# Last mixer of a graph network: row statistics in two parts, and its first work moved into the attention slots

## The chip, the cores and the metric

The kernel runs on one core of a Trainium2 chip. The time is the device time of one execution in microseconds (us), as a median of several runs. The engines are TensorE (PE in the profile, its weight loads PEld), VectorE (DVE), ScalarE (ACT), GpSimd (POOL) and SyncE (SP); each runs its own instruction stream in order, and they meet through semaphores.

## What is computed

x is (64, 128, 128) in float32: 64 batches, 128 nodes, 128 features. Four mixers follow each other, each as x = x + mixer(relu(layernorm(x))). The first is two graph convolutions and four LSTMs over windows, the second graph attention, the third masked self attention, the fourth a spectral graph network:

```python
deg = jnp.sum(A, axis=0) + jnp.sum(A, axis=1) - jnp.diagonal(A)
d_inv_sqrt = jnp.where(deg > 0, jax.lax.rsqrt(deg), 0.0)
L = jnp.diag(deg) - A
L_norm = d_inv_sqrt[:, None] * L * d_inv_sqrt[None, :]
_, U = jnp.linalg.eigh(L_norm)
agg = jnp.einsum('mn,bnd->bmd', U.T, features)
h = jax.nn.relu(agg @ W1 + b1)
out = h @ W2 + b2
return jnp.einsum('nm,bmd->bnd', U, out)
```

The eigenvectors U don't depend on x, so they are worked out beside the first three mixers: a Householder reduction to tridiagonal form, the eigenvalues by counting signs, the eigenvectors by twisted recurrences (Z), and U = QT' Y with Y the transpose of Z.

## The kernel before

X stays in SBUF, nodes on the partitions. A group is four batches, so a mixer has 16 groups (`NG`). The second and third mixer run as one pipeline of 32 groups (`GROUPS`): groups 0 to 15 are the graph attention, 16 to 31 the self attention (the text counts them 0 to 31, the profile's tiles by `g % 2`). PSUM has eight banks; an even group of the pipeline uses banks 0 to 2, an odd one 3 to 5; bank 7 serves the eigenvalues, and bank 6 is free there. The last mixer has all eight, four for each group of a pair.

The pipeline is laid out in slots S = -1 to 32 on TensorE (lines 780 to 829) and ScalarE (567 to 609). In slot S TensorE turns the exponentials of group S-1 (line 787, once ScalarE has made them), makes scores of group S+1 (lines 802 to 812), the product of probabilities and values of group S-1 (line 799) and turns the normalized input of group S+2. ScalarE in the same slot takes the exponentials of group S-1 (line 576), copies PSUM banks (lines 581 to 596), and normalizes group S+2 with `ln` (line 501, four instructions with scale `rstd` and bias `nbias`). `root(n)` (line 507) is the square root for the statistics number n; those numbered 3 and 4 stand behind slots that `ROOTS_AFTER` gives.

VectorE runs the order of `half_list` (line 154): "scores" of a group (the row maximum, line 988), "output" of a group (`add_output`, line 966: a reciprocal, four fused residual adds into X on line 974, four row statistics on line 868), and the two halves of the layer norm's statistics: `stats_1(n)` (seven operations up to 1/variance, line 870) and, after ScalarE's root, `stats_2(n)` (five, up to `rstd` and `nbias`, line 881). Statistics 3 and 4 cover half of the rows each, 5 all 64, by `COLUMNS`. In the last ten places of the list (`VECTORS`) part k of the eigenvectors, `vectors(k)` (line 1260), stands behind the place. Part 0 waits for GpSimd's twisted products (`tw_done`, line 1273), and part 5 ends in Z (`z_rdy`), behind "scores 31" and before "output 30".

Behind all slots come, in this order: the statistics of all rows in both halves and ScalarE's root between them, Z's transpose into Y, U and its transpose UT, then the last mixer in eight pairs of groups:

```python
e.wait_ge(z_rdy, 1)
e.transpose(bank[2][:, 0:P], Z[:, :], ident[:, :]).then_inc(z_ps, 1)
e.wait_ge(y_rdy, 1)
mm(bank[3][:, 0:P], QT[:, :], Y[:, :]).then_inc(u_ps, 1)
mm(bank[6][:, 0:P], Y[:, :], QT[:, :]).then_inc(u_ps, 1)
e.wait_ge(u_sb, 2)
```

A pair of the last mixer is: ScalarE normalizes both groups (line 617), TensorE multiplies by U (844), ScalarE copies (620), TensorE multiplies by W1 (847), ScalarE applies bias and ReLU (623), TensorE multiplies by W2 (850), VectorE adds a bias (1345), TensorE multiplies by UT (855), VectorE adds X (1350), SyncE writes the output (373). On each engine a step is issued for both groups before the next step.

## Time and profile before

| | us |
|---|---|
| median of 3 runs | 979.74 (978.82 to 980.7) |
| the profiled execution | 979.09 |
| its span, first to last instruction | 977.4 |
| TensorE busy | 815.5 (83%) |
| VectorE busy | 766.3 (78%) |
| ScalarE busy | 500.3 (51%) |
| GpSimd busy | 183.0 (19%) |
| mean granted clock of TensorE | 0.946 of full |

The page's first part gives each engine's busy time. A timeline gives instructions in order of time, like ones merged ("x4" is four of them; their time is from the first start to the last end): start, duration, engine, line, operation, output<-inputs, and in brackets how long the engine idled before and what released it. `T`, `bank` and the like stand without their number. A granted clock of 1.00 is TensorE's 2.4 GHz, 0.50 is 1.2 GHz. A float32 matmul is recorded twice, so a step of four matmuls has eight records, a transpose one.

### The profile page before, as it was taken

How to read it: one execution, taken by the hardware profiler on the slowest of the kernel's cores; microseconds unless marked ns; L12 is line 12 of the kernel's file. 1: busy time of each engine (PE TensorE's matmuls, PEld its weight loads, DVE VectorE, ACT ScalarE, POOL GpSimd, SP SyncE). 2: the span in 40 equal slices, each digit the busy share in tenths (PEclk: the TensorE clock that was granted, in tenths of full speed). 3: DMA queues.
4: the chain of work that ended last, by engine and by line, in shares of the span. 5: the costliest groups of instructions: out<-in, count | busy, mean ns of one | idle time of the engine just before them, and what ended most of it. 6: DMA issues, size and time to landing. Idle time of an engine off the chain costs nothing.

```text
span 977.4 us, 13714 instructions
## 1 busy us (share of the span) xinstructions
PE 815.5 (83%) x3856; PEld 542.0 (55%) x3862; DVE 766.3 (78%) x3143; ACT 500.3 (51%) x1103; POOL 183.0 (19%) x444
## 2 busy tenths in 40 slices
PE   4579988889999999898999997489954787697798
PEld 3468774344444566666555454467643565475565
DVE  6877777888888778888888788959989999867433
ACT  0037766554444434444433432268853786695575
POOL 2111111111111111111121111003122332471000
PEclk9999999999999989999999999889996898898799
DMA  8000000000000000000000000000000000000022
GB/s 291 0 1 1 2 1 1 1 1 1 1 1 1 1 1 1 1 0 1 1 1 0 1 1 0 1 1 1 1 1 0 1 1 1 1 2 1 22 72 80
DMA packets 13970, 12.17 MB, mean 12 GB/s; under 512 B 1091, under 2 KB 10822, under 8 KB 13894
## 3 DMA queue, kind: packets, MB, share of 16 engines
q1 hardware_dynamic: 10704, 8.46, 2.6%
q10 hardware_dynamic: 3190, 2.84, 0.9%
q8 instruction: 31, 0.51, 0.2%
q14 instruction: 45, 0.37, 0.1%
HBM read 7.10 MB, written 4.19 MB: 12 GB/s over the span
## 4 chain that ended last, share of the span: by engine, by line
issue 48%; DVE 24%; PE 13%; POOL 12%; ACT 2%; POOLq 0%; DVEq 0%; ACTq 0%
PE bank L628 13%; POOL col_root L407 7%; DVE tt L860 4%; DVE stat L868 3%; DVE HT L860 3%; DVE X L861 3%; DVE uu L860 2%; POOL XI L411 2%; DVE X L860 1%; DVE sm L984 1%; POOL PP L454 1%; POOL m L454 1%; POOL u L454 1%; DVE dm L860 1%; DVE sm L988 1%
## 5 line engine op out<-in xcount | busy, mean ns | idle before, releaser
L545 ACT ACTIVATE G<-bank,bias 128x512 f32<-128x512 f32 (+1 forms) x252 | 158.5, 636 | 235.0 <-PE bank L628 197.2
L628 PE MATMUL bank<-HT,wih 128*128 128x512 f32 (+1 forms) x504 | 250.3, 582 | 0.5 <-ACT HT L531 0.5
L407 POOL TENSOR_TENSOR col_root<-sa,neg_half 128x1 f32<-128x1 f32 x126 | 79.3, 629 | 485.1 <-DVE sa L862 485.1
L628 PEld LDWEIGHTS bank<-VI 128*128 128x128 f32 x506 | 94.7, 202 | 120.4 <-DVE VI L860 58.0
L628 PE MATMUL bank<-H,whh 128*128 128x512 f32 (+1 forms) x288 | 136.2, 555 | 2.6 <-DVE H L860 2.6
L628 PE MATMUL bank<-VI 128*128 128x129 f32 (+63 forms) x506 | 95.6, 273 | 22.3 <-DVE VI L860 22.2
L501 ACT ACTIVATE T<-X,nbias,rstd 128x128 f32<-128x128 f32 x256 | 104.6, 486 | 6.7 <-DVE nbias L861 6.7
L505 ACT COPY T<-bank 128x512 f32<-128x512 f32 x128 | 74.8, 584 | 55.7 <-PE bank L628 43.9
L638 PE MATMUL bank<-ident,T 128*128 128x128 f32 x256 | 42.3, 296 | 59.9 <-ACT T L576 51.2
L628 PEld LDWEIGHTS bank<-XI,A 128*128 128x128 f32 x252 | 41.1, 201 | 89.6 <-DVE A L861 87.8
L628 PEld LDWEIGHTS bank<-HT,wih 128*128 128x128 f32 x504 | 80.6, 195 | 10.0 <-issue 4.1
L628 PE MATMUL bank<-XI,A 128*128 128x2 f32 x252 | 47.2, 257 | 27.7 <-DVE A L861 26.9
L638 PEld LDWEIGHTS bank<-ident,T 128*128 128x128 f32 x256 | 31.3, 150 | 65.9 <-ACT T L576 57.2
L628 PEld LDWEIGHTS bank<-H,whh 128*128 128x128 f32 x288 | 49.1, 193 | 27.6 <-issue 20.0
L868 DVE BATCH_NORM_STATS2 stat<-X 128x6 f32<-128x128 f32 x256 | 56.4, 281 | 1.6
L538 ACT ACTIVATE T<-C 128x512 f32<-128x512 f32 (+1 forms) x72 | 41.3, 574 | 19.4 <-DVE C L860 19.3
L861 DVE SCALAR_TENSOR_TENSOR XI<-xy,bank 128x2 f32<-128x2 f32 x125 | 28.2, 225 | 24.6 <-PE bank L628 13.8
L418 POOL TENSOR_TENSOR G<-M,d 128x512 f32<-128x512 f32 (+1 forms) x16 | 23.6, 1481 | 126.6 <-DVE HT L860 94.7
L628 PE MATMUL bank<-XI 128*128 128x3 f32 x252 | 45.7, 251 | 1.5 <-issue 0.9
L860 DVE TENSOR_TENSOR tt<-HT,G 128x64 f32<-128x64 f32 (+1 forms) x128 | 43.9, 343 | 3.6
L1088 DVE TENSOR_SCALAR col_c<-sa,col_root 128x1 uint32<-128x1 uint32 x126 | 26.7, 212 | 25.1 <-POOL col_root L407 25.0
L861 DVE SCALAR_TENSOR_TENSOR A<-bank,col_q,A 128x127 f32<-128x127 f32 (+62 forms) x126 | 35.5, 282 | 12.2 <-PE bank L628 10.9
(338 smaller groups left out, 1582.3 us busy)
## 6 DMA issues: line engine op xcount, KB each, us to landing
out_x<-T SPq DMA_DIRECT2D x16, 256.0 KB, 2.3
wih<-in_WihT ACTq DMA_DIRECT2D x1, 1024.0 KB
whh<-in_WhhT ACTq DMA_DIRECT2D x1, 1024.0 KB
qkvT<-in_WqkvT ACTq DMA_DIRECT2D x1, 192.0 KB
wg<-in_Wg ACTq DMA_DIRECT2D x2, 64.0 KB
l3w<-in_L3W ACTq DMA_DIRECT2D x2, 64.0 KB
adjT<-in_adjT ACTq DMA_DIRECT2D x1, 64.0 KB
adj<-in_adj SPq DMA_DIRECT2D x1, 64.0 KB, 2.0
```

What stands on the lines that cost most here:

```text
L407: e.tensor_tensor(out=col["root"][:, :], in0=sa[:, 0:1], in1=neg_half[:, :], op=ALU.pow).then_inc(root_ready, 1)
L454: TP = lambda o, a, b, op: e.tensor_tensor(out=o, in0=a, in1=b, op=op)
L501: i = e.activation(T[g % 2][0][:, ds(b % GB * D, D)], X[:, b, :], ACT.Relu, bias=nbias[:, b:b + 1], scale=rstd[:, b:b + 1])
L505: e.copy(out=dst[:, :], in_=src[:, :]).then_inc(done, 1)
L538: e.activation(T[x.h][3][:, 0:x.n], C[x.h][:, 0:x.n], ACT.Tanh).then_inc(l_t, 1)
L545: e.activation(G[x.h][:, gate, 0:n], gate_bank(k)[:, 0:n], ACT.Tanh if gate == 2 else ACT.Sigmoid, bias=bias[:, 4 * (x.p - 1) + gate:4 * ( ...
L628: mm = lambda out, l, r, start=True, stop=True: e.matmul(out, l, r, start=start, stop=stop)
L638: i = e.transpose(dst[:, ds(b * P, P)], src[:, ds(b * P, P)], ident[:, :])
L860: TT = lambda o, a, b, op: e.tensor_tensor(out=o, in0=a, in1=b, op=op)
L861: STT = lambda o, a, s, b, o0, o1: e.scalar_tensor_tensor(out=o, in0=a, scalar=s, in1=b, op0=o0, op1=o1)
L868: return e.bn_stats(out=stat[:, b, :], in_=X[:, b, :])
L1088: link(e.tensor_scalar(c("c").bitcast(U32), sa[:, 2:3].bitcast(U32), 0x80000000, c("root").bitcast(U32), ALU.bitwise_and, ALU.bitwise_or))
```

## The change

Five things, all in the last part of the kernel:

1. The last mixer's statistics come in two halves. `stats_1(5)`, for rows 0 to 31, stands behind output 23 on VectorE, `root(5)` behind slot 25 on ScalarE, `stats_2(5)` behind output 25. Rows 32 to 63 are statistics 6: `stats_1(6)` behind output 31 as before, then `root(6)` and `stats_2(6)`.
2. ScalarE normalizes group 0 of the last mixer at the end of slot 30, group 1 at the end of slot 31. `root(6)` stands between the first pair's copies and its ReLUs, and the wait for `ln_rdy` 6 ahead of group 8.
3. TensorE transposes Z at the end of slot 30 and makes U and UT at the end of slot 31, all into bank 7. VectorE's copy to Y is now the end of part 5 of the vectors (before output 30), the copies to U and UT are part 7 (between outputs 30 and 31).
4. The last mixer's banks: an odd group has 5, 4, 6, 7 for its four steps in place of 4, 5, 6, 7; an even one has 0, 1, 2, 3 as before. This lets TensorE begin the mixer's first step behind the last slot.
5. TensorE waits for `q_x` (output 31 added) before the second step of group 1, which writes the bank that held group 31's output.

```diff
@@ -167,7 +167,11 @@
             halves.append(("stats_1", 3))
         if k == NG:
             halves.append(("stats_1", 4))
-    return halves + [("stats_1", 5)]
+        if k == NG + NG // 2 + 2:
+            halves.append(("stats_2", 5))
+        if k == NG + NG // 2:
+            halves.append(("stats_1", 5))
+    return halves + [("stats_1", 6)]
 
 
 class Group:
@@ -180,7 +184,7 @@
         return 0 <= self.k < GROUPS
 
 
-COLUMNS = {1: slice(0, B), 2: slice(0, B), 3: slice(0, B // 2), 4: slice(B // 2, B), 5: slice(0, B)}
+COLUMNS = {1: slice(0, B), 2: slice(0, B), 3: slice(0, B // 2), 4: slice(B // 2, B), 5: slice(0, B // 2), 6: slice(B // 2, B)}
 HALF = half_list()
 N_HALVES = len(HALF)
 VECTORS = 10
@@ -201,7 +205,7 @@
     return h
 
 
-for _n in (3, 4):
+for _n in (3, 4, 5):
     ROOTS_AFTER[max(S for S in SLOTS if needs(S) <= HALF.index(("stats_1", _n)) + 1)] = _n
 
 
@@ -359,6 +363,9 @@
         def at_place(x, place):
 
             return HT[:, ds(x.b0 // GB, x.gb // GB), place:place + (x.nw - 1) * x.p + 1:x.p, :]
+
+        def last_bank(g, n):
+            return bank[(5, 4, 6, 7)[n] if g % 2 else n]
 
         def gate_bank(k):
             return bank[2 + k % 5]
@@ -598,6 +605,10 @@
                     if not after.gat and after.g % (NG // 2) == 0:
                         e.wait_ge(ln_rdy, 3 + after.g // (NG // 2))
                     ln(after.g, g_h if after.gat else q_h)
+                if S == GROUPS - 2:
+                    e.wait_ge(ln_rdy, 5)
+                if GROUPS - 2 <= S < GROUPS:
+                    ln(S + 2 - GROUPS, r_h)
                 if S in ROOTS_AFTER:
                     root(ROOTS_AFTER[S])
                 for n in BLOCKS_AFTER.get(S, []):
@@ -607,20 +618,23 @@
                         e.wait_ge(sum_ps, n - 1)
                     e.wait_ge(pr_ready, products(n))
                     e.activation(sg[n % 2][:, 0:w], prod[:, 0:w], ACT.Sign).then_inc(sgn_ready, 1)
-            root(5)
-            e.wait_ge(ln_rdy, 5)
 
 
             for it in range(NG // 2):
                 pair = (2 * it, 2 * it + 1)
+                if 2 * it == NG // 2:
+                    e.wait_ge(ln_rdy, 6)
                 for g in pair:
-                    ln(g, r_h)
+                    if it:
+                        ln(g, r_h)
                 for g in pair:
                     e.wait_ge(r_s0, g + 1)
-                    copy(T[g % 2][1], bank[4 * (g % 2)], r_a)
+                    copy(T[g % 2][1], last_bank(g, 0), r_a)
+                if not it:
+                    root(6)
                 for g in pair:
                     e.wait_ge(r_s1, g + 1)
-                    e.activation(T[g % 2][2][:, :], bank[4 * (g % 2) + 1][:, :], ACT.Relu, bias=l3b1[:, 0:1]).then_inc(r_hid, 1)
+                    e.activation(T[g % 2][2][:, :], last_bank(g, 1)[:, :], ACT.Relu, bias=l3b1[:, 0:1]).then_inc(r_hid, 1)
 
         @blk.tensor
         def _(e):
@@ -821,6 +835,13 @@
                     for q in range(chunks):
                         i = mm(bank[7][:, :], identb[:, :], sg[n % 2][:, ds(512 * q, 512)], start=(b == 0 and q == 0), stop=(b == NB - 1 and q == chunks - 1))
                     i.then_inc(sum_ps, 1)
+                if S == GROUPS - 2:
+                    e.wait_ge(z_rdy, 1)
+                    e.transpose(bank[7][:, 0:P], Z[:, :], ident[:, :]).then_inc(z_ps, 1)
+                if S == GROUPS - 1:
+                    e.wait_ge(y_rdy, 1)
+                    mm(bank[7][:, ds(P, P)], QT[:, :], Y[:, :]).then_inc(u_ps, 1)
+                    mm(bank[7][:, ds(2 * P, P)], Y[:, :], QT[:, :]).then_inc(u_ps, 1)
                 if S == LAMBDA_AFTER:
                     e.wait_ge(lam_rdy, 1)
                     mm(bank[7][:, 0:P], bc(col["lam"][:, 0:1]), ident[:, :]).then_inc(lam_ps, 1)
@@ -829,11 +850,6 @@
                     mm(bank[7][:, 0:1], hist[:, :], ones[:, 0:1]).then_inc(hist_ps, 1)
 
 
-            e.wait_ge(z_rdy, 1)
-            e.transpose(bank[2][:, 0:P], Z[:, :], ident[:, :]).then_inc(z_ps, 1)
-            e.wait_ge(y_rdy, 1)
-            mm(bank[3][:, 0:P], QT[:, :], Y[:, :]).then_inc(u_ps, 1)
-            mm(bank[6][:, 0:P], Y[:, :], QT[:, :]).then_inc(u_ps, 1)
             e.wait_ge(u_sb, 2)
 
 
@@ -841,18 +857,20 @@
                 pair = (2 * it, 2 * it + 1)
                 for g in pair:
                     e.wait_ge(r_h, g + 1)
-                    each(bank[4 * (g % 2)], part(T[g % 2][0]), whole(U)).then_inc(r_s0, 1)
+                    each(last_bank(g, 0), part(T[g % 2][0]), whole(U)).then_inc(r_s0, 1)
                 for g in pair:
                     e.wait_ge(r_a, g + 1)
-                    mm(bank[4 * (g % 2) + 1][:, :], l3w1[:, :], T[g % 2][1][:, :]).then_inc(r_s1, 1)
+                    if g == 1:
+                        e.wait_ge(q_x, NG)
+                    mm(last_bank(g, 1)[:, :], l3w1[:, :], T[g % 2][1][:, :]).then_inc(r_s1, 1)
                 for g in pair:
                     e.wait_ge(r_hid, g + 1)
-                    each(bank[4 * (g % 2) + 2], part(T[g % 2][2]), whole(l3w2)).then_inc(r_s2, 1)
+                    each(last_bank(g, 2), part(T[g % 2][2]), whole(l3w2)).then_inc(r_s2, 1)
                 for g in pair:
                     e.wait_ge(r_o2, g + 1)
                     if g >= 2:
                         e.wait_ge(r_out, g - 1)
-                    mm(bank[4 * (g % 2) + 3][:, :], UT[:, :], T[g % 2][3][:, :]).then_inc(r_s3, 1)
+                    mm(last_bank(g, 3)[:, :], UT[:, :], T[g % 2][3][:, :]).then_inc(r_s3, 1)
 
         @blk.vector
         def _(e):
@@ -1323,31 +1341,31 @@
                     link(TS(c("sign"), choice, 0.0, -2.0, ALU.is_gt, ALU.mult))
                     link(TS(c("sign"), c("sign"), 1.0, None, ALU.add))
                     TS(Z[:, :], Zn[:, :], c("sign"), None, ALU.mult).then_inc(z_rdy, 1)
+                    e.wait_ge(z_ps, 1)
+                    e.tensor_copy(out=Y[:, :], in_=bank[7][:, 0:P]).then_inc(y_rdy, 1)
+
+                if part == 7:
+                    e.wait_ge(u_ps, 2)
+                    e.tensor_copy(out=U[:, :], in_=bank[7][:, ds(P, P)]).then_inc(u_sb, 1)
+                    e.tensor_copy(out=UT[:, :], in_=bank[7][:, ds(2 * P, P)]).then_inc(u_sb, 1)
 
             while halves < N_HALVES:
                 attentions(halves)
                 vectors(halves - (N_HALVES - VECTORS))
                 halves += 1
-            stats_2(5)
-            for part in range(VECTORS, 6):
-                vectors(part)
-            e.wait_ge(z_ps, 1)
-            e.tensor_copy(out=Y[:, :], in_=bank[2][:, 0:P]).then_inc(y_rdy, 1)
-            e.wait_ge(u_ps, 2)
-            e.tensor_copy(out=U[:, :], in_=bank[3][:, 0:P]).then_inc(u_sb, 1)
-            e.tensor_copy(out=UT[:, :], in_=bank[6][:, 0:P]).then_inc(u_sb, 1)
+            stats_2(6)
 
 
             for it in range(NG // 2):
                 pair = (2 * it, 2 * it + 1)
                 for g in pair:
                     e.wait_ge(r_s2, g + 1)
-                    TT(half4(T[g % 2][3]), half4(bank[4 * (g % 2) + 2]), b2rep[:, :].unsqueeze(1).to_broadcast([P, GB, P]), ALU.add).then_inc(r_o2, 1)
+                    TT(half4(T[g % 2][3]), half4(last_bank(g, 2)), b2rep[:, :].unsqueeze(1).to_broadcast([P, GB, P]), ALU.add).then_inc(r_o2, 1)
                 for g in pair:
                     e.wait_ge(r_s3, g + 1)
                     if g >= 2:
                         e.wait_ge(out_done[g % 2], 16 * (g // 2))
-                    TT(half4(T[g % 2][5]), half4(bank[4 * (g % 2) + 3]), X[:, ds(g * GB, GB), :], ALU.add).then_inc(r_out, 1)
+                    TT(half4(T[g % 2][5]), half4(last_bank(g, 3)), X[:, ds(g * GB, GB), :], ALU.add).then_inc(r_out, 1)
 
 
 # ---- launch ----
```

## Rows read from the trace of the kernel before

**Rows 1.** The page, busy times of each engine over the span.
```profile
PE 815.5 (83%) x3856; PEld 542.0 (55%) x3862; DVE 766.3 (78%) x3143; ACT 500.3 (51%) x1103; POOL 183.0 (19%) x444
```

**Rows 2.** Timeline of VectorE, groups 23 to 27: start, us, instruction [idle before <-releaser].
```profile
855.23 1.13 DVE L861 SCALAR_TENSOR_TENSOR X<-bank,sm,X 128x128 f32<-128x128 f32 x4 [3.09 <-PE bank L628]
...
878.18 0.87 DVE L868 BATCH_NORM_STATS2 stat<-X 128x6 f32<-128x128 f32 x4
...
882.77 0.22 DVE L862 TENSOR_SCALAR PP<-PP 128x108 f32<-128x108 f32 x1 [3.71 <-POOL PP L454]
```

**Rows 3.** Timeline of VectorE, Z and the output of group 30.
```profile
901.34 0.29 DVE L862 TENSOR_SCALAR Z<-Zn,col_sign 128x128 f32<-128x128 f32 x1
...
901.75 1.13 DVE L861 SCALAR_TENSOR_TENSOR X<-bank,sm,X 128x128 f32<-128x128 f32 x4
...
902.91 0.87 DVE L868 BATCH_NORM_STATS2 stat<-X 128x6 f32<-128x128 f32 x4
```

**Rows 4.** Timeline of VectorE, statistics of all rows, then Y and U.
```profile
906.10 0.27 DVE L860 TENSOR_TENSOR mean<-stat 128x64 f32<-128x64 f32 x1
...
910.11 0.28 DVE L1335 COPY Y<-bank 128x128 f32<-128x128 f32 x1
...
911.71 0.29 DVE L1337 COPY U<-bank 128x128 f32<-128x128 f32 x1 [1.31 <-PE bank L628]
```

**Rows 5.** Timeline of ScalarE, group 31 to the second pair of the last mixer.
```profile
897.97 0.37 ACT L576 ACTIVATE T<-bank,sm 128x128 f32<-128x128 f32 x1 [1.00 <-DVE sm L988]
...
908.34 0.26 ACT L509 ACTIVATE rootv<-var 128x64 f32<-128x64 f32 x1 [5.78 <-DVE var L879]
...
910.22 3.19 ACT L501 ACTIVATE T<-X,nbias,rstd 128x128 f32<-128x128 f32 x8 [1.62 <-DVE nbias L861]
...
917.10 0.69 ACT L623 ACTIVATE T<-bank,l3b 128x512 f32<-128x512 f32 x1 [0.45 <-PE bank L628]
...
917.96 0.69 ACT L623 ACTIVATE T<-bank,l3b 128x512 f32<-128x512 f32 x1 [0.17 <-PE bank L628]
...
918.54 3.17 ACT L501 ACTIVATE T<-X,nbias,rstd 128x128 f32<-128x128 f32 x8
...
926.01 3.18 ACT L501 ACTIVATE T<-X,nbias,rstd 128x128 f32<-128x128 f32 x8
```

**Rows 6.** Timeline of TensorE, groups 30 and 31, Y's products, first pair.
```profile
895.70 0.60 PE L638 MATMUL bank<-ident,T 128*128 128x128 f32 x4
...
897.03 1.16 PE L628 MATMUL bank<-C,T 128*128 128x128 f32 x8 [0.73 <-ACT T L505]
...
899.53 1.11 PE L638 MATMUL bank<-ident,T 128*128 128x128 f32 x4 [1.34 <-ACT T L576]
...
901.32 2.07 PE L628 MATMUL bank<-C,T 128*128 128x128 f32 x8 [0.67 <-ACT T L505]
...
910.45 0.80 PE L628 MATMUL bank<-Y,QT 128*128 128x128 f32 x2 [6.84 <-DVE Y L1335]
...
912.25 3.79 PE L628 MATMUL bank<-U,T 128*128 128x128 f32 x16 [0.58 <-DVE UT L1338]
```

**Rows 7.** Timeline of ScalarE, the root for rows 32 to 63 of an earlier mixer.
```profile
790.35 1.28 ACT L509 ACT_TABLE_LOAD   x1
...
792.90 0.23 ACT L509 ACTIVATE rootv<-var 128x32 f32<-128x32 f32 x1 [1.27 <-DVE var L879]
...
793.14 1.28 ACT L576 ACT_TABLE_LOAD   x1
```

**Rows 8.** Timeline of VectorE, first and last operation of stats_1 at 32 columns.
```profile
791.09 0.21 DVE L860 TENSOR_TENSOR mean<-stat 128x32 f32<-128x32 f32 x1
...
792.51 0.35 DVE L879 RECIPROCAL var<-var 128x32 f32<-128x32 f32 x1
```

**Rows 9.** Windows of 2 us: busy PE, PEld, DVE, ACT, POOL, then PEclk, DMA.
```profile
914.00:916.00 2.00, 2.00 (x11) 2.00 (x11) 0.00 (x0) 0.59 (x1) 0.00 (x0) 0.50 0.00 0
...
916.00:918.00 2.00, 2.00 (x6) 0.70 (x5) 0.00 (x0) 1.31 (x3) 0.00 (x0) 0.94 0.00 0
```

## The prediction

> **What bounds the kernel now.** I read the views in this order: the busy times, then VectorE's timeline over the last slots, ScalarE's and TensorE's over the same stretch, and last two stretches of the windows view for TensorE's clock. The busy row [rows 1] says only that no engine is full over the whole span. The change touches the last 120 us, so what a step is worth is read from there.
>
> VectorE in the slots has slack: before the residual add of group 23 it idles 3.09 us [rows 2]. At 879.05 (start 878.18 plus 0.87) it ends the row statistics of group 27 and then sits 3.71 us until 882.77, waiting for GpSimd's twisted products (`tw_done`) [rows 2]. From 882.77 it works without a gap through parts 0 to 5 of the eigenvectors, group by group, until Z is written at 901.63 (901.34 plus 0.29), and then does the outputs of groups 30 and 31 (from 901.75 to the end of the last statistics, two times 2.04 to 2.3 us) [rows 3]. So VectorE is the bound between 882.8 and 908.3.
>
> Then everything is in series. VectorE computes the first half of the statistics of all 64 rows (906.10 to 908.3), ScalarE takes the root (908.34), VectorE finishes rstd and nbias and copies Y (910.11), TensorE forms U and its transpose, VectorE has U at 911.71 [rows 4, 5]. ScalarE normalizes groups 0 and 1 from 910.22 to 913.41. TensorE meanwhile gives Y's products at 910.45 and starts the last mixer at 912.25, at half its clock: 3.79 us for 16 matmul records [rows 6]. The ReLU of group 0 starts at 917.10, that of group 1 at 917.96, the normalization of groups 2 and 3 at 918.54, and one pair later the same operation stands at 926.01, 7.47 us on [rows 5]. From 918.54 on the mixer is a repeating chain in which nothing is changed but bank numbers. So the whole effect of the change is how far 918.54 moves.
>
> **The change, part by part.**
>
> *Statistics of rows 0 to 31, early.* `stats_1(5)` on VectorE behind output 23 and `stats_2(5)` behind output 25, with `root(5)` at the end of slot 25 on ScalarE. At 32 columns `stats_1` takes 1.77 us (791.09 to 792.86) [rows 8]; `stats_2` is no longer than its 64-column form, 908.6 to 910.1, 1.5 us [rows 4, 5]. Both fit in VectorE's idle time (3.09 us ahead of one output, 3.71 us at the wait for GpSimd) [rows 2]. ScalarE has no such room: it and TensorE hand over to each other in each slot. The root brings a table load, the root, and a load back: 1.28, 0.24, 1.28 us by the rows of the same step ahead of group 16's half of the rows (790.35, 792.90, 793.14) [rows 7]; with gaps 2.85 us. There the root itself waited for VectorE; here its input is there in time, since `stats_1(5)` would end near 859.1 (855.23 + 2.04 + 1.77) [rows 2, 3, 8], before ScalarE is through slot 25. The exponentials of groups 25 to 28, the products and outputs behind them come 2.85 us later. VectorE then ends group 27 at 879.05 + 2.85 = 881.9 instead of 879.05, still 0.85 us ahead of 882.77 [rows 2]. GpSimd's chain, which ends that wait, has all its inputs earlier, so this costs nothing. Bounds: 0, and, if VectorE's 12 added small operations hold up GpSimd, some tenths (I allow 0.3). Without that cover it would be 2.85 us on the path.
>
> The Trainium skill, "ScalarE: Activation LUTs", section "What ACT_TABLE_LOAD costs", says that a switch of table costs a drain beside the load, some 2.66 us in all. By that the pair of switches would be 5.3 us, 1.6 us more than the cover. The rows here disagree: the load back starts 0.01 us behind the root [rows 7].
>
> *Z's transpose, Y and U within the slots.* TensorE now waits for Z at the end of slot 30. It would get there by 895.7, where the trace has it turn group 30's probabilities [rows 6], so it stands until 901.63, some 6 us: the turn and product of group 30, which were hidden beside part 5 of the vectors, go onto the path. Queued behind that wait are, on TensorE, all of slots 31 and 32; on ScalarE the copy of the turned probabilities, then the new normalization of group 1 and the exponentials of group 31; on VectorE outputs 30 and 31. TensorE was down to its half clock even with less idle time (899.53: a turn 1.11 us, against 0.60 at 895.70; a product 2.07 against 1.16) [rows 6], so I start at half. Step by step:
>
> - Z's transpose, one record of the four in a turn of 1.11, with latency: 0.45. To 902.1. VectorE's copy to Y (0.28, [rows 4]) lies beside the next step.
> - Turn of group 30: 1.11. To 903.2. ScalarE's copy up to TensorE's next start: 0.68 (900.64 to 901.32) [rows 6]. To 903.9.
> - ScalarE: normalization of group 1, half of 3.19 for eight, 1.6; exponentials of group 31 until TensorE's turn, 897.97 to 899.53, 1.56 [rows 5, 6]. To 907.0.
> - TensorE beside it: product of group 30, 2.07, then Y's two products, 910.45 to 911.71, 1.26 [rows 4, 6]. To 907.2. This ends last, by little. VectorE's output 30 (2.04) and the copies of U and UT end near 908.7, out of the way.
> - Turn of group 31, copy, product, release of VectorE: 1.11 + 0.68 + 2.07 + 0.1 = 3.96 at half clock, 0.60 + 0.68 + 1.16 + 0.1 = 2.54 at full. I take the turn at half and the product at full, 3.05, since TensorE is then busy nearly all the time since 903.9 and a comparable run of work (912.25 to 915.8 in the trace) is what preceded the rise there [rows 6, 9]. To 910.3.
> - Output 31, 901.75 to 903.78: 2.04 [rows 3]. To 912.3.
> - `stats_1(6)`, 32 columns: 1.77 [rows 8]. To 914.1. The root: 0.25 with latency. ReLU of group 0 at 914.3.
>
> Beside it TensorE has the last mixer's first step (U, 1.9 us for a pair at full clock, by half of the 3.79 [rows 6]): 910.2 to 912.1. ScalarE copies, loads the table by 914.0, just in time. ReLU of group 1 0.58 behind, groups 2 and 3 another 0.58 behind (917.96 to 918.54) [rows 5]: 915.45. `stats_2(6)` lies beside the product of the hidden layer, and its result is first needed by group 8.
>
> So 918.54 becomes 915.45: 3.1 us less. As a balance: from the end of output 31 to the first ReLU the trace has 11.0 us (906.1 to 917.10), the new order 2.0, since half the statistics, U, the first pair's normalization and the mixer's first step are off that stretch. That is 9.0 less. Output 31 itself ends 6.2 later (912.3 for 906.1). And the pair's two ReLUs stand 0.58 apart and not 0.86, since both wait for the root and not for TensorE: 0.3 more. Nothing is late next: `u_sb` is there near 908.7, `q_x` before group 1's second step.
>
> *Ends of the unknown terms.* Full clock already for group 31's turn: ReLU at 913.8, gain 3.6. Half clock through group 31 and the pair's first step: the product ends at 911.0, U's products at 914.8, ScalarE's copy and the load behind it at 916.7, ReLU at 917.0, gain 0.3. These two, with the 0.3 of GpSimd, make the range of the sum.
>
> **How the profiled execution stands to the runs.** It took 979.09 us, 977.4 of it span; the median of three is 979.74, the spread 1.9. I take the difference from the median: 979.74 - 3.1 = 976.6. About 0.2% (2.0 us) is what a measurement of this kernel can tell from no change.
>
> **The rivals.**
>
> *A: the clock comes back late.* TensorE comes out of 6 us without work and then has two to four us at a time, with gaps. For: in the trace the records of 899.53 to 912.25 are all at half, and the stretch 914 to 916 is granted 0.50 [rows 6, 9]. Against: from 903.2 to 910.4 of that it had nothing to do. If it rises only with the mixer's first step, the gain is 0.3 to 1.3: 978.4 to 979.4. Chance 0.15.
>
> *B: slower.* The same mechanism further on: the clock is at half through the whole first pair. The mixer's three further steps then take up to twice their time; the two of them behind the ReLU (a pair in 3.79, by the row of U, and not in 1.9, each [rows 6]) add 3.8 us, less the 0.3 gained: 979.74 + 3.5 = 983.2. It decides once the clock is still at half when the first ReLU ends, near 917.7. Against: in the trace the clock was back in the stretch 916 to 918 (0.94) behind work without a gap since 912.25 [rows 6, 9], and here the like work begins near 909. Chance 0.07.
>
> *C: the cover of the early root is too short.* Of 3.71 us 0.85 are left over. If the root costs 5 us or more of ScalarE's slot instead of 2.85, or VectorE's added operations hold GpSimd up by over 1 us, the gain is 1.5 to 2: 978 and a little. For: it is a narrow margin, and ScalarE passes each delay to all slots. Against: rows 7. Chance 0.10.
>
> *D: handovers.* Eight handovers between engines stand on the new chain from Z to the first ReLU, and I gave them 0.05 to 0.1 each. VectorE's wait for U's products in the trace shows what they can add: TensorE's two starts at 910.45 and VectorE's copy at 911.71 [rows 4, 6]. With 0.25 more on each the gain is 1.1: 978.6. Chance 0.05.
>
> The forecast has 0.63: 975.9 to 977.7.
>
> **The numbers.** Range 975.4 to 979.7: it takes in the forecast, A, C and D and leaves out B and some of the tails. Faster by over 0.2% (below 977.8): 0.64. Within: 0.28 (A, C, D and the weak end of the forecast). Slower by over 0.2%: 0.08.
>
> **What would show it.** VectorE's wait for GpSimd ahead of the second pivots should shrink from 3.71 to near 0.9, still ended by GpSimd at 882.8, with Z at 901.6. TensorE should show one record at 901.7 after some 6 us without work, group 30's turn behind it, the exponentials of group 31 near 905.4 (were 897.97), output 31 on VectorE at 910.3 (was 6 us earlier), the first ReLU near 914.3, the normalization of groups 2 and 3 near 915.4, and pairs 7.4 us apart as before. The prediction is wrong if Z comes later than 902, if records of the mixer's first step are still at half clock, or if the pairs' distance has changed.

## The result, and the profile after

The changed kernel takes 978.46 us (median of 20 runs), the kernel before 980.48 beside it: a ratio of 0.9981, 95% interval 0.9973 to 0.9989, so 1.9 us less (1.1 to 2.6). The forecast was 3.1 less. That is the right side, inside the range, and about 60% of the size; it lies on the line between "faster" and "within 0.2%".

The spans of the two profiled executions are nearly equal (977.4 before, 977.3 after), because the changed kernel's is 1.7 us late long before the first instruction that was changed: VectorE ends the eigenvalue (`lam`, line 1226 of the kernel before) at 842.57 before and at 844.23 after. Over all profiled executions of this study that instruction starts between 839.8 and 847.3. Everything the change touches lies behind it, so I measure the **last part**: from this instruction's start to the end of the span. It is 134.83 us before and 133.07 after, 1.76 less, in line with the timed runs. All times "from lam" below have this origin. VectorE's timeline of the kernel before at this place and at output 31 (the fused residual add), then of the changed one:

```profile
842.57 0.22 DVE L861 SCALAR_TENSOR_TENSOR col_lam<-col_frac,col_w,col_lo 128x1 f32<-128x1 f32 x1
...
904.03 1.13 DVE L861 SCALAR_TENSOR_TENSOR X<-bank,sm,X 128x128 f32<-128x128 f32 x4
```

```profile
844.23 0.22 DVE L879 SCALAR_TENSOR_TENSOR col_lam<-col_frac,col_w,col_lo 128x1 f32<-128x1 f32 x1
```

VectorE after (timeline; start, duration, instruction, idle time before it). These answer to [rows 2 to 4]:

```profile
884.14 0.22 DVE L880 TENSOR_SCALAR PP<-PP 128x108 f32<-128x108 f32 x1 [1.03 <-POOL PP L461]
...
902.82 0.29 DVE L880 TENSOR_SCALAR Z<-Zn,col_sign 128x128 f32<-128x128 f32 x1
...
907.35 1.13 DVE L879 SCALAR_TENSOR_TENSOR X<-bank,sm,X 128x128 f32<-128x128 f32 x4 [3.30 <-PE bank L642]
...
912.06 1.13 DVE L879 SCALAR_TENSOR_TENSOR X<-bank,sm,X 128x128 f32<-128x128 f32 x4 [2.07 <-PE bank L642]
```

The wait for GpSimd is 1.03 us, was 3.71; Z comes 58.59 from lam, was 58.77. Then VectorE waits 0.57 for Z's transpose, 3.30 for group 30's product and 2.07 for group 31's, where before it ran through. Output 31 starts 67.8 from lam, was 61.5.

ScalarE after, against [rows 5, 7]: the early root between its two table loads, then the mixer's first pair.

```profile
863.16 1.28 ACT L516 ACT_TABLE_LOAD   x1
864.45 0.23 ACT L516 ACTIVATE rootv<-var 128x32 f32<-128x32 f32 x1
864.70 1.28 ACT L583 ACT_TABLE_LOAD   x1
866.00 0.37 ACT L583 ACTIVATE T<-bank,sm 128x128 f32<-128x128 f32 x1
...
914.99 0.59 ACT L512 COPY T<-bank 128x512 f32<-128x512 f32 x1 [0.71 <-PE bank L642]
915.60 1.28 ACT L516 ACT_TABLE_LOAD   x1
916.89 0.23 ACT L516 ACTIVATE rootv<-var 128x32 f32<-128x32 f32 x1
917.03 1.25 ACT L637 ACTIVATE T<-bank,l3b 128x512 f32<-128x512 f32 x2
918.17 3.18 ACT L508 ACTIVATE T<-X,nbias,rstd 128x128 f32<-128x128 f32 x8
...
925.92 3.18 ACT L508 ACTIVATE T<-X,nbias,rstd 128x128 f32<-128x128 f32 x8
```

TensorE after, against [rows 6], and a window of 2 us against [rows 9] (busy PE, PEld, DVE, ACT, POOL, then the granted clock):

```profile
867.55 0.66 PE L652 MATMUL bank<-ident,T 128*128 128x128 f32 x4 [2.25 <-ACT T L583]
868.05 1.11 PE L642 MATMUL bank<-T,mqk 128*128 128x512 f32 x2
...
903.16 0.47 PE L840 MATMUL bank<-ident,Z 128*128 128x128 f32 x1 [7.06 <-DVE Z L880]
903.42 1.06 PE L652 MATMUL bank<-ident,T 128*128 128x128 f32 x4
905.16 2.08 PE L642 MATMUL bank<-C,T 128*128 128x128 f32 x8 [0.68 <-ACT T L512]
...
908.09 1.11 PE L652 MATMUL bank<-ident,T 128*128 128x128 f32 x4
909.88 2.08 PE L642 MATMUL bank<-C,T 128*128 128x128 f32 x8 [0.68 <-ACT T L512]
911.75 3.21 PE L642 MATMUL bank<-U,T 128*128 128x128 f32 x16
...
921.55 1.95 PE L642 MATMUL bank<-U,T 128*128 128x128 f32 x16
```

```profile
914.00:916.00 2.00, 2.00 (x10) 1.29 (x10) 1.67 (x8) 1.27 (x3) 0.00 (x0) 0.90 0.04 8
```

Z's transpose follows 7.06 us without work. From there to the mixer's first step every record is at half clock (1.2 GHz): turns 1.06 and 1.11, products 2.08, the first step 3.21. The clock is 0.50 in the window from 912 and back in the one from 914 (0.90).

### The profile page after: what moved, and what is told of

Read it like the earlier page. It is cut to its first block, busy times and chain, and to the rows that moved or that the text cites. A ratio compares the mean times of both kernels' runs of the same rounds, so it can differ in the third digit from the quotient of the medians.

```text
span 977.3 us, 13729 instructions
## 1 busy us (share of the span) xinstructions
PE 814.0 (83%) x3856; PEld 541.6 (55%) x3862; DVE 768.1 (79%) x3155; ACT 502.1 (51%) x1106; POOL 182.7 (19%) x444
## 3 DMA queue, kind: packets, MB, share of 16 engines
q10 hardware_dynamic: 3190, 2.84, 0.9%
## 4 chain that ended last, share of the span: by engine, by line
issue 48%; DVE 24%; PE 13%; POOL 12%; ACT 2%; POOLq 0%; DVEq 0%; ACTq 0%
PE bank L642 13%; POOL col_root L414 7%; DVE tt L878 4%; DVE stat L886 3%; DVE HT L878 3%; DVE X L879 2%; DVE uu L878 2%; POOL XI L418 2%; DVE X L878 1%; DVE sm L1002 1%; POOL PP L461 1%; POOL m L461 1%; POOL u L461 1%; DVE sm L1006 1%; POOL t L461 1%
```

## Experiments

Each kernel was timed beside the kernel before, in five rounds. The table gives the ratio with its interval and, for the profiled execution, the last part, which has none of the scatter of the first 840 us. Most readings below rest on the latter; one execution each, but the stages in them repeat: VectorE comes past the wait for GpSimd at 39.9 to 40.4 from lam in all but the one kernel made to miss it, and from the mixer's first ReLU to the end it is 60.2 to 60.4 us in all thirteen. So the last part is decided by when the first ReLU starts, and a difference of 0.3 us or less between two kernels says nothing.

| kernel | ratio to before (95%) | last part, us | against before |
|---|---|---|---|
| before | 1 | 134.83 | |
| changed | 0.9981 (0.9973 to 0.9989) | 133.07 | -1.76 |
| e1, products behind the slots | 0.9979 (0.9965 to 0.9993) | 133.17 | -1.66 |
| e2, products in the slots only | 1.0068 (1.0049 to 1.0088) | 139.90 | +5.07 |
| e3, changed + table early | 0.9958 (0.9940 to 0.9975) | 132.37 | -2.46 |
| e4, changed + TensorE kept busy | 0.9963 (0.9947 to 0.9980) | 130.32 | -4.51 |
| e5, before + 8 constants | 0.9990 (0.9974 to 1.0007) | 134.62 | -0.21 |
| e6, Z behind the last slot | 0.9964 (0.9946 to 0.9982) | 130.40 | -4.43 |
| e7, changed, early root dearer | 1.0017 (1.0000 to 1.0034) | 136.25 | +1.42 |
| e8, e6 + table early + 4 constants | 0.9931 (0.9907 to 0.9955) | 128.89 | -5.94 |
| e8b, e6 + table early | 0.9953 (0.9936 to 0.9970) | 130.16 | -4.67 |
| e9, before + 10 constants | 0.9996 (0.9983 to 1.0008) | 133.22 | -1.61 |
| e10, e8 + 2 constants | 0.9916 (0.9902 to 0.9929) | 127.54 | -7.29 |

### e1 and e2: the two halves of the change, one at a time

e1 takes the changed kernel and puts Z's transpose, Y, U and UT behind the slots again:

```diff
-                if S == GROUPS - 2:
-                    e.wait_ge(z_rdy, 1)
-                    e.transpose(bank[7][:, 0:P], Z[:, :], ident[:, :]).then_inc(z_ps, 1)
-                if S == GROUPS - 1:
-                    e.wait_ge(y_rdy, 1)
...
+            e.wait_ge(z_rdy, 1)
+            e.transpose(bank[7][:, 0:P], Z[:, :], ident[:, :]).then_inc(z_ps, 1)
+            e.wait_ge(y_rdy, 1)
...
             e.wait_ge(u_sb, 2)
```

(and VectorE's three copies behind `stats_1(6)`). e2 is the kernel before with only that block moved the other way, into the slots, and the copies into parts 5 and 7.

> The change without its move of Z's transpose, Y, U and UT: these are made behind the last slot again (statistics in two halves, both early normalizations and the new banks stay). Theory (the split and the early normalization bring the gain, the wait for Z inside the slots takes part of it back): by the rows of the kernel before, Y's products at 908.3, U at 910.1, the first step at half clock until 913.9, table load until 915.8, the normalization of groups 2 and 3 at 917.3 and not 918.54: 1.2 us less than before, so 0.8 more than the changed kernel. Rival 1 (the wait for Z inside the slots is what costs, and without it the rest is worth far more): 3 us or more below before. Rival 2 (the early root on ScalarE is not covered by VectorE's wait for GpSimd): no gain or slower than before.

> The kernel before with only the move of Z's transpose, Y, U and UT into the slots; statistics of all rows and their root at the end, no early normalization. Theory (TensorE's wait for Z puts turn and product of group 30 on the path): output 31 ends about 5 to 6 us later and the whole kernel takes 5 to 6 us more than before. Rival (the wait costs little, since TensorE was idle there anyway): within 1 us of before, or 1.5 us less by the hidden products.

e1 has a last part 1.66 us shorter than before, the changed kernel 1.76; the ratios are 0.9979 and 0.9981. So the move of Z's products into the slots brings nothing that can be told (0.1 us). The theory had expected a loss of 0.8; the first step took 3.43 us and not 3.8. Rival 1 (that without the wait the rest is worth 3 us) did not come either, but not because the wait is cheap: e1 gives the time back in another place. VectorE copies Y only behind the statistics, and TensorE waits 4.44 us for it:

```profile
907.51 0.79 PE L642 MATMUL bank<-Y,QT 128*128 128x128 f32 x2 [4.44 <-DVE Y L1348]
...
909.31 3.43 PE L642 MATMUL bank<-U,T 128*128 128x128 f32 x16 [0.58 <-DVE UT L1351]
```

e6 below differs from e1 in nothing but the place of VectorE's three copies, and there rival 1 holds. How the 1.66 us divide between the statistics in halves and the early normalization, no run shows.

e2 is 5.07 us longer, 5 to 6 expected. TensorE of e2:

```profile
906.52 0.47 PE L826 MATMUL bank<-ident,Z 128*128 128x128 f32 x1 [5.72 <-DVE Z L864]
906.79 1.06 PE L638 MATMUL bank<-ident,T 128*128 128x128 f32 x4
908.52 2.08 PE L628 MATMUL bank<-C,T 128*128 128x128 f32 x8 [0.68 <-ACT T L505]
...
911.25 0.83 PE L638 MATMUL bank<-ident,T 128*128 128x128 f32 x4
912.76 1.16 PE L628 MATMUL bank<-C,T 128*128 128x128 f32 x8 [0.68 <-ACT T L505]
922.01 3.62 PE L628 MATMUL bank<-U,T 128*128 128x128 f32 x16 [8.09 <-ACT T L501]
```

As in the changed kernel, TensorE is idle 5.72 us until Z, group 30's turn and product follow at half clock, and VectorE stands 3.30. Here nothing uses the time: the statistics come 5.6 us later (output 31 at 67.0 from lam, was 61.5), and the first step waits 8.09 us for the normalization. So in the changed kernel the wait costs what the early work behind it earns. One thing differs: TensorE does the same work in the same order from Z's transpose on, but in e2 the clock is back within group 31's turn (0.83, and the product 1.16), in the changed kernel and in e3 only in the mixer's first step.

### e3: the table load out of the way

```diff
+            e.activation(early[:, :], half[:, :], ACT.Sqrt)
             for it in range(NG // 2):
                 pair = (2 * it, 2 * it + 1)
```

> The changed kernel with one square root of a constant column on ScalarE behind its last slot, so that the table is loaded in idle time ahead of the first pair's copies. Theory (the load behind the second copy, 915.60 to 916.88 in the changed kernel's trace, held the root up by 0.95 us; the ReLUs then wait for TensorE's second step): 0.8 us less than the changed kernel. Rival (TensorE at half clock alone decides, the load is hidden by it): no change. Second rival (the statistics decide): the root would still be at 916.9.

The last part is 0.70 us shorter than the changed kernel's (0.8 expected).

```profile
907.39 1.28 ACT L624 ACT_TABLE_LOAD   x1
...
913.47 0.23 ACT L517 ACTIVATE rootv<-var 128x32 f32<-128x32 f32 x1 [0.44 <-DVE var L899]
```

The load lies in idle time at 907.39. The root no longer stands behind copy and load: ScalarE idles 0.44 us for VectorE, and the root starts 71.94 from lam (72.66 in the changed kernel). So the statistics are what is late next, as the second rival said, but it starts 0.7 us earlier and not at the old time.

### e4, e5, e9: TensorE given work while it waits

```diff
                 if S == GROUPS - 2:
+                    for _f in range(8):
+                        mm(bank[6][:, :], ident[:, :], whh[:, 0, :, :].rearrange("p g o -> p (g o)"))
                     e.wait_ge(z_rdy, 1)
```

e5 and e9 put eight and nine of the same in the kernel before, between Z's transpose and the wait for Y; e9 one more (into bank 5) ahead of the wait for U.

> The changed kernel with eight matmuls of constants into the unused bank 6 ahead of TensorE's wait for Z, about 7 us of work in its 7.06 us of idle time; their results are not used. Theory (the clock is what made the gain 1.9 and not 3.1 or more: turns of 1.11 and not 0.60, products of 2.08 and not 1.16, the first step 3.21 and not 1.95): turn and product of groups 30 and 31 come at full clock, output 31 ends 1.9 us earlier, the first ReLU 2.8 us earlier: 2.5 to 2.8 us less than the changed kernel. Rival (the order of the waits decides, TensorE's records are beside others): less than 0.5 us.

> The kernel before with the same eight matmuls of constants into bank 6, in TensorE's 6.84 us of idle time between Z's transpose and Y's products. Theory of the clock: Y's products in 0.6 and not 1.2 us, the first step in 1.95 and not 3.79, the normalization of groups 2 and 3 about 1.7 us earlier, so 1.5 to 1.7 us less than before. Rival (ScalarE's normalization of the first pair decides): no change. If it gains as much as the same work gains in the changed kernel, the clock explains none of the difference between the two kernels, only their common level.

> The kernel before with ten matmuls of constants in TensorE's idle time: nine ahead of its wait for Y, one ahead of its wait for U (with eight ahead of Y alone the clock had fallen again at 914, in the middle of the first step). Theory (the clock is worth as much in the kernel before, where the first step is fed by ScalarE's normalization, as the first step's records say): the first step follows the normalizations, ReLU of group 0 1.7 us earlier, 1.7 us less than before. In the changed kernel the same work was worth 2.75 us of the last part. So of the 1.3 us between forecast and result the clock explains about 1. Rival (the clock is worth 2.5 us or more here too): then it is a common level, and the order explains the difference. Rival (no gain): the normalization decides.

e4's last part is 2.75 us shorter than the changed kernel's, as the theory of the clock said (TensorE, then VectorE at output 31):

```profile
894.06 7.03 PE L642 MATMUL bank<-whh,ident 128*128 128x512 f32 x16
...
901.44 0.60 PE L652 MATMUL bank<-ident,T 128*128 128x128 f32 x4
...
905.64 0.66 PE L652 MATMUL bank<-ident,T 128*128 128x128 f32 x4 [1.32 <-ACT T L583]
...
907.97 1.95 PE L642 MATMUL bank<-U,T 128*128 128x128 f32 x16
```

```profile
908.24 1.13 DVE L881 SCALAR_TENSOR_TENSOR X<-bank,sm,X 128x128 f32<-128x128 f32 x4 [1.62 <-PE bank L642]
```

Turns are 0.60 and 0.66 us, products 1.16, the first step 1.95, and output 31 starts 1.8 us earlier (66.06 from lam). Group 31's turn still idles 1.32 us before, now for its exponentials: the normalization of group 1, which was put ahead of them, is what is late next.

e5 did not test what it was meant to. TensorE's last constant ended at 910.2, U's products had their short records (0.49 and 0.39), but the first step was slow again, and the gain is 0.21.

```profile
903.20 7.03 PE L628 MATMUL bank<-whh,ident 128*128 128x512 f32 x16
911.67 0.49 PE L628 MATMUL bank<-Y,QT 128*128 128x128 f32 x2 [1.44 <-DVE Y L1337]
...
913.25 3.52 PE L628 MATMUL bank<-U,T 128*128 128x128 f32 x16 [0.86 <-ACT T L501]
```

```profile
912.00:914.00 2.00, 1.14 (x10) 0.98 (x9) 0.49 (x2) 2.00 (x6) 0.00 (x0) 0.96 0.00 0
914.00:916.00 2.00, 2.00 (x10) 1.75 (x10) 0.00 (x0) 1.23 (x3) 0.00 (x0) 0.50 0.03 8
```

The clock was 1.00 until 912 and 0.50 in the window from 914: it fell behind gaps of 1.44 and 0.86 us between short pieces, in spite of 7 us of work ahead of them. In e9 the first gap is 0.60 us and the second is gone, the clock is 1.00 from 894 on, and the first step comes in two pieces of 1.13 and 1.16 with a wait of 0.32 for ScalarE's normalization between them:

```profile
911.73 1.13 PE L628 MATMUL bank<-U,T 128*128 128x128 f32 x8
913.17 1.16 PE L628 MATMUL bank<-U,T 128*128 128x128 f32 x8 [0.32 <-ACT T L501]
```

The last part is 1.61 shorter (1.7 expected). The timed ratio shows none of it (0.9996; the interval reaches from 1.7 us less to 0.8 more), so by the timed runs this stays open; by the traces the clock is worth 1.6 us in the kernel before and 2.75 in the changed one, where it also sets turns and products of groups 30 and 31.

### e6, e8b, e8, e10: Z's products behind the last slot

```diff
-                if S == GROUPS - 2:
-                    e.wait_ge(z_rdy, 1)
...
+            e.wait_ge(z_rdy, 1)
...
+
+                if part == 6:
                     e.wait_ge(z_ps, 1)
                     e.tensor_copy(out=Y[:, :], in_=bank[7][:, 0:P]).then_inc(y_rdy, 1)
 
-                if part == 7:
+                if part == 8:
                     e.wait_ge(u_ps, 2)
```

That is e6: TensorE's block is where e1 has it, but VectorE copies Y behind output 30, and U and UT behind output 31, ahead of the statistics. e8b adds e3's line, e8 four constants besides (two at the end of slot 31, two ahead of the wait for U), e10 two more ahead of the wait for Y.

> The changed kernel with Z's transpose and Y's products behind TensorE's last slot; VectorE copies Y behind output 30, U and UT behind output 31 (before the statistics of the second half). Theory (TensorE's wait for Z in front of group 30's turn costs about 6 us of output 31's end and is the largest loss of the change): output 31 ends near 906.4 on the scale of the kernel before, U is there at 906.9, the first step at half clock until 910.8, table load until 912.6, normalization of groups 2 and 3 at 914.0: 4.5 us less than before, 2.5 less than the changed kernel. Rival (clock): the first step is as slow as before, so no more than 1 us below the changed kernel.

> The kernel with Z behind the slots and the table loaded early, without matmuls of constants. Theory (in the version without the early load the ReLU of group 1 already waited for TensorE's second step at half clock, 910.75 in its trace): the load is worth 0 to 0.2 us here, and the 1.5 us between that version and the one with both come from the clock. Rival (the load is what counts): 1.0 to 1.5 us below the version with Z behind the slots.

> The kernel with Z behind the slots, the table loaded early by a root of a constant, and four matmuls of constants in TensorE's idle time (two at the end of slot 31, two ahead of the wait for U). Theory: beyond the 4.5 us of the version without these two, the load (0.5 to 0.8) and part of the first step's half clock (up to 1.9) come off: 5.2 to 6.5 us less than before. Rival (the statistics of the second half, about 2.0 us behind output 31, then decide and end near 908.9, and TensorE at half clock in spite of the constants): 4.5 to 5 us less.

> As the version with Z behind the slots, early load and four matmuls of constants, with two more of them ahead of the wait for Y, so that TensorE has no longer stretch without work before the first step. Theory (the clock fell at 907.9 in that version's trace, behind 2.0 us without work): the first step takes 1.95 and not 2.80 us and starts 0.5 us earlier, the ReLU of group 1 is 1.4 us earlier: 7.3 us less than before, 1.4 less than that version. Rival (the statistics of the second half now decide, root near 66 us behind the eigenvalue): 0.5 to 1 us less than that version.

e6's last part is 4.43 us shorter than before (4.5 expected), 2.67 shorter than the changed kernel's and 2.77 shorter than e1's, so both places count: TensorE's wait for Z behind the last slot, and VectorE's copies ahead of the statistics. Output 31 starts 61.67 from lam, 0.2 later than before and 6.2 earlier than in the changed kernel. The clock didn't help: the first step takes 3.78 us, as in [rows 6]. TensorE, VectorE and ScalarE of e6:

```profile
904.08 3.78 PE L642 MATMUL bank<-U,T 128*128 128x128 f32 x16 [1.45 <-DVE UT L1350]
```

```profile
901.47 1.13 DVE L877 SCALAR_TENSOR_TENSOR X<-bank,sm,X 128x128 f32<-128x128 f32 x4
```

```profile
910.75 0.69 ACT L637 ACTIVATE T<-bank,l3b 128x512 f32<-128x512 f32 x1 [0.15 <-PE bank L642]
```

The ReLU of group 1 (910.75) waits for TensorE, not for the root, so an early load has little to give: e8b gains 0.24 over e6 (0 to 0.2 expected). The four constants of e8 give 1.27 over e8b; the first step still takes 2.80:

```profile
906.27 0.49 PE L644 MATMUL bank<-Y,QT 128*128 128x128 f32 x2 [2.03 <-DVE Y L1352]
...
909.35 2.80 PE L644 MATMUL bank<-U,T 128*128 128x128 f32 x16
```

With six (e10) it takes 2.05, the granted clock is 1.00 in every window from 860 to the end, and the last part is 7.29 us shorter than before (7.3 expected; the ratio of 0.9916 says 8.2, 7.0 to 9.6). e10 is faster than both kernels. TensorE of e10:

```profile
911.51 2.05 PE L644 MATMUL bank<-U,T 128*128 128x128 f32 x16 [0.24 <-DVE UT L1359]
```

### e7: the cover of the early root

```diff
                     root(ROOTS_AFTER[S])
+                if S == 25:
+                    e.activation(early[:, 0:1], half[:, :], ACT.Exp)
+                    e.activation(early[:, 1:2], half[:, :], ACT.Sqrt)
```

> The changed kernel with a further exponential and a further square root of constants behind the early root, so that ScalarE loads tables four times and not twice there (about 3.0 us more in slot 25). Theory (the early root is covered by VectorE's wait for GpSimd, of which 1.03 us are left in the changed kernel's trace): 2.0 us more than the changed kernel, and VectorE's wait for GpSimd gone. Rival (ScalarE's delay of the slots is on the path one to one): 3.0 us more. Second rival (slack elsewhere absorbs it): no change.

The last part is 3.18 us longer than the changed kernel's, not 2.0. At first sight that is the rival ("one to one"). The trace (TensorE, ScalarE, VectorE) says otherwise:

```profile
870.72 1.11 PE L656 MATMUL bank<-ident,T 128*128 128x128 f32 x4 [5.26 <-ACT T L584]
871.63 1.91 PE L646 MATMUL bank<-T,mqk 128*128 128x512 f32 x2
```

```profile
874.06 1.65 ACT L509 ACTIVATE T<-X,nbias,rstd 128x128 f32<-128x128 f32 x4
```

```profile
887.47 0.22 DVE L884 TENSOR_SCALAR PP<-PP 128x108 f32<-128x108 f32 x1
```

ScalarE's addition is 3.0 us (the exponentials start 5.84 behind the first load and not 2.84). TensorE waits 5.26 us for them and comes out at half clock: the turn and the product behind it take 1.11 and 1.91 us, where the changed kernel had 0.66 and 1.11 behind a wait of 2.25. ScalarE then idles 1.12 us at a copy, and its next normalization starts 10.74 us behind the first table load and not 6.51: 4.2 us late and not 3.0. Less 1.03 of cover that is 3.2, and VectorE's wait for GpSimd is gone (887.47 has none). The cover is real, and it is 1 us deep.

## Why the forecast was right or wrong

The forecast has the sign, and the time lies in its range, but the path to it is not the one it described. Two of its own signs of being wrong came: records of the mixer's first step were still at half clock, and the first two pairs stand 7.75 us apart. (The third, Z later than 902, came only on the span's scale; from lam Z is on time.) The number is inside the range since that was priced as rival A; the sum of 3.1 came out 1.3 too high, and by these steps:

- **Part one, the early root costs nothing: right.** 2.84 us on ScalarE (863.16 to 866.00; 2.85 was worked out), VectorE's wait for GpSimd shrank to 1.03 (near 0.9), and Z stands 0.2 us earlier from lam. GpSimd was not held up (VectorE comes past the wait at 39.9 from lam, 40.2 before). e7 shows both the cover and its depth. Of the two prices for the switch of tables, the rows hold again: 864.70 is 0.02 us behind the end of the root. By the Trainium skill, "ScalarE: Activation LUTs", section "What ACT_TABLE_LOAD costs", each switch of table has a drain of about 1.38 us beside the load; as an estimate from that figure, the exponentials would have come some 2.8 us later than they did. The trace doesn't agree, and the measurement decides.
- **The chain from Z to group 31's turn: right, 0.6 too long.** 5.57 us forecast (901.63 to 907.2), 4.98 measured (903.11 to 908.09). Both branches, ScalarE's exponentials and TensorE's products, end within 0.1 us of each other, as worked out.
- **Group 31's turn and product: wrong.** Turn at half clock and product at full gave 3.05; both were at half, 3.97 (908.09 to 912.06). 0.9 lost. This was the choice between two ends, 3.96 and 2.54, and the upper one came, nearly to the digit. The step that failed is the return of the clock: the work since 903.9 was taken as enough for it, and it wasn't. It wasn't far off either: in e2, with the same work of TensorE, it was (turn 0.83, product 1.16). So a forecast of one of the two ends is in part a matter of luck here.
- **The root behind the first pair's copies: wrong.** "Loads the table by 914.0, just in time" hung on the first step at full clock. It took 3.21, so copy, load and root stood in series (914.99, 915.60, 916.89), and the root came 1.0 us behind the statistics' end at 915.91. e3 gets 0.7 of it back.
- **The pair's ReLUs, 0.3 us: wrong in kind.** The balance booked as gain that they stand 0.58 and not 0.86 apart. They do, but the second pair is not 7.47 behind but 7.75 (918.17 to 925.92); from there on the pairs are 7.43 apart in both kernels. From the first ReLU to the second pair's first step are 4.54 us before (917.10 to 921.64) and 4.52 after (917.03 to 921.55): TensorE sets it. The yardstick should have been the first ReLU, and "from 918.54 on nothing is changed" was the wrong line to draw.
- **The sum.** 3.1 forecast, + 0.6 (chain) + 0.2 (Z from lam earlier), - 0.9 (turn and product), - 1.0 (load), - 0.3 (pair): 1.7. The last part has 1.76.
- **The rivals.** What happened is rival A, with the clock back in the mixer's first step; its price, 0.3 to 1.3, was too low for two reasons: the 0.6 of the chain, and a first step of 3.21 and not 3.79, since the clock came back within it. B did not come. C did not come, and e7 shows that it was 1 us away. D (handovers of 0.25 more each) did not come either: the copy steps took 0.68 as in the rows.
- **What the prediction did not ask.** It took the order of the change as given and priced it. e1 and e2 show what that hid: the products in the slots and their wait come out even (0.1 us), and the gain is that of the statistics in halves and the early normalization. Its own sentence, that output 31 ends 6.2 us later, named a loss twice as large as the gain it forecast. That should have raised the question which instruction could stand elsewhere.

## What to carry to other kernels

Put a wait for another engine's result where the waiting engine's queue has nothing left that others need: the same instructions behind the last slot (e6) gave 2.7 us that the wait in front of group 30's turn had cost. It takes both ends: with TensorE's part moved and VectorE's copies left behind the statistics (e1) nothing was gained. When a step leaves the path, look at what TensorE's idle time turns into: matmuls of constants in the gaps were worth 2.75 us (e4), and 2.6 us in the better order (e10 against e8b), which together with it made 7.3. Measure a late change from an instruction just ahead of it, since the 840 us before it scatter by more than the effect.

## What the runs showed of the hardware

TensorE's clock can fall without a long idle stretch. In e5 it was at 0.50 by 914 after 7.03 us of unbroken work until 910.2, with gaps of 1.44 and 0.86 us and two short pieces between; in e8 it was half at 908 after a gap of 2.03 us, and in e10, where that gap was filled, it stayed at full. But gaps of this size don't always do it: e4 had 1.32 us ahead of group 31's turn and 0.68 on both sides of it and stayed at 1.00, and of three kernels with the same instructions up to this turn, and 1.34 to 1.45 us of idle time ahead of it, the one before turned group 31 at half clock (1.11) and e5 and e9 at full (0.66). What decides, these runs don't show. Where the clock was at half when the mixer's first step began, it came back in the first or second step (the first took 3.12 to 3.79 us in the kernel before, the changed one, e1, e2, e3, e6 and e8b; in e5 and e8 the clock fell on the way to it or within it, 3.52 and 2.80; in e4 and e10 it had not fallen, 1.95 and 2.05).

A delay on one engine can cost more than itself: in e7, 3.0 us on ScalarE made TensorE wait 5.26 us and not 2.25, and ScalarE, behind TensorE's records at half clock, was another 1.2 us late.

ScalarE's table load runs ahead of the wait of the instruction that needs it, but not ahead of the instructions before it: in the kernel before it ran at 901.28, 7 us ahead of its root at 908.34 [rows 5], in the changed kernel at 915.60, behind the second copy, and in e3 at 907.39, behind group 31's copy. ScalarE's timeline before:

```profile
901.28 1.28 ACT L509 ACT_TABLE_LOAD   x1
```
